# Router's SiLU as tanh, a logistic and a product: from two ScalarE instructions to four, plus two on VectorE

## What is computed

```
def _mlp_ln(s, W1, b1, W2, b2, g, b):
    h = jax.nn.silu(s @ W1 + b1) @ W2 + b2
    return _ln(h, g, b)
```

## Time and profile before

| | |
|---|---|
| Median of 3 runs | 2436.07 us (2430.98 to 2436.33) |
| Profiled execution | 2425.26 us, its span 2423.5 us |
| PE busy | 2034.9 us (84%) |
| DVE, ACT, POOL busy | 1314.9, 1013.5, 860.7 us |
| Mean granted clock of PE | 0.905 of full speed |

### The profile page before, as it was taken

The page is one execution under the profiler, slowest core; times in us unless marked ns, Lnnn a source line. Parts: engine busy times, 40 slices in busy tenths (PEclk is TensorE's granted clock), DMA queues, the critical chain, the costliest instruction groups (busy, mean ns, idle before and its releaser), DMA issues. The chain is left out here.

```text
span 2423.5 us, 33861 instructions
## 1 busy us (share of the span) xinstructions
PE 2034.9 (84%) x11838; PEld 1292.7 (53%) x11838; DVE 1314.9 (54%) x3698; ACT 1013.5 (42%) x2503; POOL 860.7 (36%) x594
## 2 busy tenths in 40 slices
PE   6508789889888888888888888899999498989897
PEld 5305455555554555555465455457778355555545
DVE  2356857757767767767677563422111255555635
ACT  2005546636546545555555555422222141424241
POOL 0172626436447346346356240131000251515131
PEclk9659898888889899999999989899999799999998
DMA  7100021021021030030030040234355320202000
GB/s 263 46 0 21 1 73 27 1 90 27 1 90 27 1 108 9 4 104 10 18 99 1 26 124 1 72 119 145 127 183 183 111 72 18 72 15 74 9 22 19
DMA packets 67453, 146.09 MB, mean 60 GB/s; under 512 B 16356, under 2 KB 42074, under 8 KB 62946
## 3 DMA queue, kind: packets, MB, share of 16 engines
q1 hardware_dynamic: 51434, 93.79, 11.4%
q0 software_dynamic: 15872, 50.35, 7.1%
HBM read 114.64 MB, written 29.46 MB: 59 GB/s over the span
## 5 line engine op out<-in xcount | busy, mean ns | idle before, releaser
L1263 ACT ACTIVATE att_buf<-att_buf,nmin 128x384 f32<-128x384 f32 (+3 forms) x512 | 289.1, 565 | 393.7 <-DVE nmin L1628 393.3
L1041 PE MATMUL bank<-kk,qT 32*128 32x512 f32 (+2 forms) x1024 | 285.6, 602 | 40.7 <-DVE nmin L1628 40.3
L778 POOL TENSOR_TENSOR big<-ex_at,kx 128x2048 f32<-128x2048 f32 x64 | 236.2, 3718 | 151.7 <-DVE xt_na L1373 113.5
L1074 PE MATMUL bank<-ident,att_buf 128*128 128x128 f32 x1280 | 224.3, 302 | 60.7 <-ACT att_buf L1271 60.0
L1271 ACT COPY att_buf<-bank 128x384 f32<-128x384 f32 (+3 forms) x512 | 211.5, 413 | 22.6 <-PE bank L1088 20.8
L725 POOL TENSOR_TENSOR big<-kx 128x1280 f32<-128x1280 f32 x64 | 162.6, 2575 | 158.8 <-ACT kx L1161 142.4
L1617 DVE TENSOR_TENSOR att_buf<-bank,wdiag 128x128 f32<-128x128 f32 x384 | 93.0, 284 | 223.1 <-PE bank L1046 221.8
L1088 PE MATMUL bank<-att_buf,vp 128*32 128x128 f32 x2560 | 209.3, 298 | 0.0
L1074 PEld LDWEIGHTS bank<-ident,att_buf 128*128 128x128 f32 x1280 | 155.9, 155 | 81.8 <-ACT att_buf L1263 79.9
L790 POOL DMA_INDIRECT buf_d<-nB,sidx x64 | 62.5, 977 | 355.2 <-DVE sidx L1492 338.1
L1041 PEld LDWEIGHTS bank<-kk,qT 32*128 32x128 f32 x1024 | 97.8, 200 | 117.7 <-DVE nmin L1628 66.0
(11 more groups left out here) (352 smaller groups left out, 3982.8 us busy)
## 6 DMA issues: line engine op xcount, KB each, us to landing
big<-in_eW SPq DMA_DIRECT2D x16, 1024.0 KB, 7.6
kk<-in_eW SPq DMA_DIRECT2D x16, 1024.0 KB, 7.7
buf_d<-zero SPq DMA_DIRECT2D x8, 640.0 KB, 7.7
xt_na<-in_xT SPq DMA_DIRECT2D x8, 512.0 KB, 3.4
nA<-in_xN SPq DMA_DIRECT2D x8, 512.0 KB, 3.6
x_d<-x SPq DMA_DIRECT2D x8, 512.0 KB, 3.3
x<-x_d SPq DMA_DIRECT2D x8, 512.0 KB, 4.3
out<-qf SPq DMA_DIRECT2D x8, 512.0 KB, 2.9
```

The lines of the kernel that those rows point to most:

```text
L778: pool.tensor_tensor(pv[:, c * P:(c + 1) * P, :].rearrange("p (h d) o -> p o h d", d=DH), spread(ex[:, t, :, 8 * c:8 * c + 8], 3, DH), spr ...
L1041: pe.matmul(bank[u % 2][:, 0:n], qT[r:r + 32, g, i * P:(i + 1) * P], kk[r:r + 32, g, T * i * P:T * i * P + n], start=True, stop=False)
L1074: mm = pe.transpose(bank[3 + u % 2][:, j * P:(j + 1) * P], pr[:, u % NPR, j * P:(j + 1) * P], ident[:])
L1263: act.activation(pr[:, u % NPR, 0:n], pr[:, u % NPR, 0:n], ACT.Exp, scale=-1.0, bias=nmin[:, u % 4:u % 4 + 1], accum_out=rsum[:, i, h:h + ...
```

## The change

The SiLU of v = u + b (u is what PE left in the bank, b the bias) is computed as (u + b) times (0.5 tanh((u + b)/2) + 0.5).

- On DVE in slot -5: two more instructions for each row b3, a memset of `half` (128x1) to 0.5 and `half_b` (128x2), half the bias. Both signal `half_ok`.
- On ACT in slot 24: instead of two SiLUs, two Tanh out of the banks into `aT3`, then two Identity in place, from SBUF to SBUF, with scale 0.5 and bias 0.5. Each Identity waits for the Tanh of its half. ACT first waits for `half_ok`.
- On DVE in a new slot `gate`, 26 (27 in `LAST`): waits for each Identity and multiplies: `aT3 = (bank + b) * aT3`, 128x512 each. These now signal `u_ok`, for which PE's `y` waits; before, the SiLUs did.

```diff
-      "s": 14, "s_out": 15, "u": 16, "silu": 24, "y": 28, ...
+      "s": 14, "s_out": 15, "u": 16, "silu": 24, "gate": 26, "y": 28, ...
-LAST = {**PLACES, ... "u": 14, "silu": 26, "y": 28, ...
+LAST = {**PLACES, ... "u": 14, "silu": 26, "gate": 27, "y": 28, ...
...
+                half_b = sb("half_b", [P, K2])
+                half = sb("half", [P, 1])
...
+                                    yield AT["silu"]
+                                    act.wait_ge(s("half_ok"), 2)
                                     for o in range(K2):
-                                        yield AT["silu"]
                                         act.wait_ge(s("u_mm"), o + 1)
-                                        act.activation(aT3[:, o, :], bank[SIDE[o]][:], ACT.Silu, bias=pc3[:, 6 + o:7 + o]).then_inc(s("u_ok"), 1)
+                                        act.activation(aT3[:, o, :], bank[SIDE[o]][:], ACT.Tanh, bias=half_b[:, o:o + 1], scale=0.5)\
+                                            .then_inc(s("tanh_ok"), 1)
+                                    for o in range(K2):
+                                        act.wait_ge(s("tanh_ok"), o + 1)
+                                        act.activation(aT3[:, o, :], aT3[:, o, :], ACT.Identity, bias=half[:, 0:1], scale=0.5).then_inc(s("gate_ok"), 1)
...
                                     done(dve.tensor_copy(pc3[:], pcol[:, b3, :]))
+                                    dve.memset(half[:], 0.5).then_inc(s("half_ok"), 1)
+                                    dve.tensor_scalar(half_b[:], pcol[:, b3, 6:6 + K2], 0.5, None, ALU.mult).then_inc(s("half_ok"), 1)
...
+                                    yield AT["gate"]
+                                    for o in range(K2):
+                                        dve.wait_ge(s("gate_ok"), o + 1)
+                                        dve.scalar_tensor_tensor(aT3[:, o, :], bank[SIDE[o]][:], pc3[:, 6 + o:7 + o], aT3[:, o, :],
+                                                                 ALU.add, ALU.mult).then_inc(s("u_ok"), 1)
                                     yield AT["y_in"]
```

More of the change, by code:

```diff
@@ L44 @@
       "kx": 0, "h1b": 1, "var2": 2, "sd2": 3, "t": 3, "t_out": 3, "h2": 4, "h2a": 6, "h2b": 7, "h": 12, "h_out": 13,
-      "s": 14, "s_out": 15, "u": 16, "silu": 24, "y": 28, "y_in": 32, "var3": 33, "sd3": 33, "f1": 34,
+      "s": 14, "s_out": 15, "u": 16, "silu": 24, "gate": 26, "y": 28, "y_in": 32, "var3": 33, "sd3": 33, "f1": 34,
       "f": 37, "f_out": 37, "r": 42, "r_in": 46, "r_exp": 47, "r_sum": 48, "pick": 49, "pos": 52, "place": 54, "rows": 58,
@@ L50 @@
       "turn1": 55, "turn1_out": 55, "c": 57, "c_out": 58}
-LAST = {**PLACES, "h": 8, "h_out": 9, "s": 11, "s_out": 12, "u": 14, "silu": 26, "y": 28, "y_in": 32, "var3": 36, "sd3": 37, "f1": 38,
+LAST = {**PLACES, "h": 8, "h_out": 9, "s": 11, "s_out": 12, "u": 14, "silu": 26, "gate": 27, "y": 28, "y_in": 32, "var3": 36, "sd3": 37, "f1": 38,
         "f": 40, "f_out": 41, "r": 42, "r_in": 46, "r_exp": 47, "r_sum": 48, "pick": 49, "pos": 52, "place": 54, "rows": 58}
```

## The result

| | before | after |
|---|---|---|
| Median of 4 runs | 2433.53 us (2430.22 to 2436.33) | 2394.13 us (2389.98 to 2401.86) |
| Ratio of the runs, 95% interval | | 0.9842 [0.9812, 0.9873] |
| Profiled execution, its span | 2425.26, 2423.5 us | 2401.86, 2400.1 us |
| Mean granted clock of PE | 0.905 | 0.909 |

The profiled execution is the longest of the four; the spans of the other three are 2388.2, 2390.5 and 2394.2 us.

What follows compares the result with a forecast made beforehand. PE, busy 84% of the span, bounds the kernel, so only its idle or slow time pays. Seven SiLUs at 3.0 us less 1.9 in the last iteration give 19.1: 2436.1 to 2417 us, range 2403 to 2441.

Steps and rivals of the forecast that it cites:

- ACT's block: Two Tanh and two Identities at the SiLU take 2.40 us instead of 3.87, with no table loads: 1.47 us gained.
- The step called the weakest: At the SiLU, PE's clock stays at 1.00 behind the shortened wait, so values take 0.85 and first-half `y` 1.99 us.
- cover of 0.85 us: DVE's biases of units 30 and 31 finish at T = 6.65, before PE's scores after `y` need them at 7.5.
- The drain of 1380 ns: Skill's added cost per ACT table load; an estimated 2.8 us more per block, 19 us over seven; the prediction doubted it.
- The last iteration: Beside the experts PE has nothing else to do, so `y` starts 1.9 us later: a loss.
- the clock's term of the sum: Per SiLU beside an attention, 1.63 us gained because values and first-half `y` no longer run at the slow clock.
- 7 x 3.0 - 1.9: Seven SiLUs beside an attention gain 3.0 us each, the last iteration loses 1.9: 19.1 us in total.
- (b): Rival: the period absorbs the gain, 3.0 us given back elsewhere at half clock; about 2436 us, chance 0.15.
- (c): Rival: shifted by 3 us, the rest of the iteration falls into the bad clock pattern; 8 us slower, 2444, chance 0.14.
- (e): Rival: more than forecast, first SiLUs gain 3.9 us and early periods settle sooner; 2408 us, chance 0.08.
- (d): Rival: Tanh and Exp each still need a table load, block 4.97 us; 10 us slower, 2446, chance 0.04.
- (a): Rival: the clock falls all the same behind the SiLU's wait, leaving 1.47 us each; 8.4 us faster, 2428, chance 0.17.

Runs made afterwards that it cites:

- e6: Kernel before with the SiLU in slot 23 instead of 24, arithmetic unchanged, on another chip: 2428.34 us, ratio 0.9841.
- e11: Changed kernel, unedited, one more execution for its trace on the chip of the filled-wait run: 2393.9 us.
- e2: Changed kernel plus a useless 1664-column copy on ACT behind the Identities, putting the wait back: 2441.77 us, ratio 1.0048.
- e3: Kernel before with SiLU kept and only DVE's two products added behind the SiLUs: 2432.22 us, ratio 1.0026.
- e4: Changed kernel, but the last iteration keeps its two SiLUs and has no product: 2390.69 us, ratio 0.986.
- e1: Kernel before with Tanh in the SiLU's place, no Identity and no product: 2391.65 us, ratio 0.986.
- e9: Kernel before with four useless 128x256 matmuls per batch row put into PE's wait at the SiLU: 2405.19 us, ratio 0.9897.
- e10: Kernel before, unedited, one more execution for its trace on the chip of the filled-wait run: 2431.76 us.
- e12: Kernel before with SiLU in slot 23 and two useless matmuls in pair 36, where PE waited for ACT: 2372.38 us, ratio 0.9761.
- e8: Changed kernel, unedited, run once more on another chip: 2434.71 us, ratio 0.9877.

## Why the prediction was right, and where it failed

**Right, to a tenth of a microsecond: what happens at the SiLU.** ACT's block 2.38 (forecast 2.40), the transposes at T = 3.48 (3.52), PE's idle time 0.88 (1.04), values at 4.69 (4.72), `y` at 5.47 for 1.99 (5.57), the next scores at 7.39 (7.5). The step called the weakest, that the clock stays at 1.00, held at six of the seven places (3.4 us of slow time there, before 30.7); at the second the first half of `y` took 3.48. The product on DVE was taken at 0.684 and takes 0.746, between the bounds, for two 1.41; its cover of 0.85 us sufficed. The drain of 1380 ns for each load that the Trainium skill has (ScalarE: Activation LUTs, What ACT_TABLE_LOAD costs) has no place here either: the loads of e6 stand as close as those of the earlier trace rows, 1.28 + 1.26 + 1.28 of the 3.87 from 417.17 to 421.04. The last iteration lost 2.05 in its wait (1.9), and some more by the clock behind it.

**Failed: the clock's term of the sum.** "Sum. 7 x 3.0 - 1.9" counts the clock only where I had seen it, behind the SiLU's wait: 1.63 us each, 11.4 in all. The account by the traces, from the first `y` to the eighth:

- the shorter waits, six of them in the stretch: 6 x 1.51 = 9.1
- slow time at the SiLUs, within the stretch 28.0 to 3.4: 24.6 / 2 = 12.3
- slow time elsewhere in the periods, 184.3 to 143.4: 40.9 / 2 = 20.5
- the last iteration's wait: -2.0

Together 39.9, measured 40.2. The forecast has the first two and the last: over all seven places they come to 10.6 + 13.7 - 2.0 = 22.3, forecast 19.1. The third, nearly as large as these together, the sum put at nothing without giving a reason. It is not made by anything the change does at those places. See the same matmuls some 53 us behind the fifth `y`, where PE waits 1.16 us for DVE in both kernels. Timeline of before, then of after:

```profile
1189.31 1.94 PE L821 MATMUL bank<-ident,xt_na 128*128 128x128 f32 x8 [1.16 <-DVE pe L1471]
1191.18 2.08 PE L1041 MATMUL bank<-kk,qT 32*128 32x512 f32 x4
```

```profile
1162.75 1.06 PE L823 MATMUL bank<-ident,xt_na 128*128 128x128 f32 x8 [1.16 <-DVE pe L1485]
1163.74 1.13 PE L1043 MATMUL bank<-kk,qT 32*128 32x512 f32 x4
```

The wait is equal, what follows is not: 1.94 and 2.08 at half the clock before, 1.06 and 1.13 after. A period has one such wait, and the clock is low behind it at six of six in before, in both executions; in after at two of six, in e11 at three of six. In before's fifth period such falls come 19, 53, 81, 108 and 173 us behind `y`; in after's fifth only 17 and 102 us behind it. Before has these same five falls in its third, fourth and fifth periods, whose lengths agree to 0.06 us; after misses some, in one period others than in the next. What in the new rhythm spares them isn't shown.

**The rivals.** (b) and (c) had seen that the rest of the period reacts to a shift, and that before's steady 174.1 looked as if the clock held it. But they let it only take, and had a chance of 0.29. (e), which has the sign that came true, spoke of the early periods alone, had 2408 and a chance of 0.08. The trace of before did not exclude the other way: 212.3 us of its stretch ran at the low clock, 184.3 of them away from the SiLU, and these could be gained as well. (d) and (a) fell with the loads and with the 1.99.

**Between the stretch and the whole.** In the profiled pair 40.2 us are gained in the stretch, but all that lies behind it, layer 1 above all, takes 809.6 in place of 795.4, and what lies ahead 2.6 more: 23.4 in all. Behind the eighth `y` no instruction is changed, but the slow time there is 115.6 instead of 87.3, worth 14.1. Whether the change costs something here stays open: off the second chip the five traces of kernels with the product on DVE (after, e2, e3, e4, e11) take 802 to 810 us in this part, the five without it (before, e1, e9, e10, e12) 795 to 800. So some 7 us of the difference come again (806.0 in e11, 799.3 in e10), and the rest may be spread. The medians, 39 us apart, and the spans of e10 and e11, 37.9 apart, show more of the stretch's gain than the first profiled pair does.

**Open.** Why the clock falls behind some equal waits and not behind others, and so how much a given shift brings, isn't settled. e1, with the shortest wait, keeps 180.9 us of slow time at a steady 170.7 a period; after has less with a longer wait. On the other chip after's stretch takes 1190.9 us with 198.0 at the low clock; its ratio is alike, but for want of a trace of before from there it isn't known what the gain is made of. Where that chip's waits of 2.2 us come from isn't known. Slots other than 23 and 24 weren't tried.

## What to carry to other kernels

When PE's clock falls behind a wait, price the wait by the matmuls that follow it and not by its own length, and give the gain a wide upper side: the falls elsewhere in the loop can go or come too, here nearly as much again as at the place itself; these runs show no rule for it. To find out how much of a wait is the clock, put matmuls of no use into it: 25 us came from that here, with the wait for ACT unchanged. Before adding instructions to be rid of a table load, look for a slot in which the load is covered: here one digit gave the same 1.6%.

## Of the hardware, what was not expected

- A wait of 1.62 us was followed by a fall of the clock at six of seven places (`y` 3.65 instead of 1.99 at the first), and one of 1.41 by another (16 values 1.92 instead of 1.07); one of 1.16 at six of six places in before and at two of six in after. Those of 0.88 at the SiLU were followed by one at 4 of 28 places (after, e4, e8, e11), those of 0.71 and 0.30 at none of 14 (e9, e1). Removing such waits, or filling them, was worth 1.0 to 2.4% of the kernel.
- Matmuls of no use made the kernel faster: 13.7 us of them gained 25 us (e9).
- The falls of before are no noise. Three of its periods agree to 0.06 us, and 174.1 comes back in another execution (e10). Those of after lay elsewhere on another chip (e8).
- An Identity from SBUF to SBUF with a bias column takes 0.724 us at 128x512, longer than Tanh out of a bank (0.691); the product of a bank and a tile takes 0.746.
- One chip of those used takes 1.6% longer for the same kernel, with waits of PE of 2.2 us in the trace of after (15.1 us in all) whose cause the trace doesn't show.
